# Where the four extra graph heads of a two-layer graph and product-key network stand: rounds 2, 4, 6, 8 in place of rounds 1 to 4

## The chip, the cores and the metric

The kernel runs on one core of one Trainium2 chip. The metric is the device time of one execution in microseconds, as the median of several runs; lower is better. The engines are TensorE (PE; its weight loads are shown apart as PEld), VectorE (DVE), ScalarE (ACT), GpSimd (POOL) and SyncE (SP).

## The reference

A residual stream x of 2048 rows by 128 goes through four blocks, each fed by a layer norm. The change concerns the first two alone.

```python
# 1. graph attention, 4 heads of 32, over the whole 2048 x 2048 adjacency
h = (x @ W).reshape(n, heads, head_dim)
e = src[:, :, None] + dst.T[None, :, :]
e = jnp.where(e > 0, e, ALPHA * e)
attn = softmax(where(adj > 0, e, NEG_INF));  out = layernorm(attn @ h) * gamma + beta
# 2. product keys: top 16 of 128 by top 16 of 128, then the top 16 of the 256 pairs, for each of 8 heads
k = jnp.einsum('bnhk,bnhkd->bnhd', kv_scores, keys_table[ind])
v = jnp.einsum('bnhk,bnhkd->bnhd', kv_scores, values_table[ind])
# causal attention of 8 heads of 128 over those k and v, then @ Wo
# 3. a second graph mix with one score per node; 4. a routed two-layer network of 32 experts
```

## The kernel before, in words

The 2048 rows are 16 tiles of 128. Four kinds of work belong to a tile.

**Graph heads.** Four heads a tile, numbered 4 x tile + s. A head is shown on PE (`show_head`, lines 755 and 756, eight matmuls into the PSUM tile wide), bent on ACT (line 962), reduced on DVE (`graph_logits`, line 1172), exponentiated on ACT (line 968), then transposed and multiplied on PE (`sum_head`: transposes at line 696, copies on ACT at line 910, products at line 705). After a tile's fourth head the tile is closed (`close_graph` on DVE: a compare over the next adjacency tile at line 1374, then a layer norm, a sum and a second layer norm, line 1089). `turn_xn1` on PE (line 850) turns the normed rows, and ACT copies them to xn1T.

**Picks.** For each tile four steps of key products (PE line 799) and two top-16 searches (DVE, `pick_keys`, `pick_pairs`, `pick_rows`, `pick_weights`). They need that tile's xn1T and give the row numbers idxT of its gather.

**Gathers.** POOL fetches the chosen table rows of a tile with 128 indirect DMAs (line 626). Four of them fill one slot of `ring`, a buffer of four slots. Two slots are a *pair*; a tile has 16 pairs. PE multiplies a slot by its weights (`sum_pair`, line 677) and so frees it, and only then may POOL fill the slot again. So POOL can be two pairs ahead of PE and no more.

**Attention.** Tile q attends to tiles 0 to q-1 in the steps, two of the eight heads in each (PE line 812, DVE line 1200, ACT line 1011, PE lines 696 and 705), and to itself in `own_keys`.

The order on every engine is written out by one plan, `plan_steps`, which all five engines walk in the same order. After a start that works on tiles 0 to 2, round n (n from 1 to 15) holds: the own keys of tile n-1, four steps that do the attention of tile n and the picks of tile n+1, and an end item. Its 16 pairs of gathered rows are those of tile n. Each step may also carry one graph head (`g`). Heads 12 to 63 are placed in rounds 1 to 12: four a round in the four steps, and in four rounds a fifth in a step of its own, the *extra step*, which stands ahead of the four and has no attention and no picks. `counts` says which of a step's three places takes a pair: in a round with an extra step the four steps take 2, 2, 2 and 3 pairs and the extra step 2, in a round without one they take 2, 3, 3 and 3; the own keys take 2 and the end item 3 in every round.

Where the fourth head of a tile stands in step s = 3, its closing is done inside the next round's own keys (`close=s < 3`, `left`). Where it stands in an earlier step or in the extra step, an end item without any pair follows that step at once, and the closing is done there:

```python
        g_end = g // 4 if g is not None and g % 4 == 3 else None
        if g_end is not None or k_end is not None or any(end):
            add("end", end, (1,), g=g_end if close else None, k=k_end)
```

In such an end item PE shows the next head first, which waits for line 1374 of the closing, and then waits for the last norm at `turn_xn1`:

```python
                if it["ahead"] is not None:
                    show_head(it["ahead"])
                if g is not None:
                    turn_xn1(g)
```

Of the kernel before, what the change touches and what calls it, by code (L numbers as in the profile page):

```python
# [22 lines left out]
def plan_steps(tiles):  # L23

    items, pending, count = [], [], dict(pair=0, kept=0, heads=0, met=0)

    def add(kind, fetch, turn_at, **what):  # L30
        item = dict(kind=kind, fetch=[], turn={}, kept=count["kept"], heads=count["heads"], met=count["met"], **what)
        for place, wanted in enumerate(fetch):
            if place in turn_at:
                item["turn"][place] = list(pending)
                count["kept"] += len(pending)
                pending.clear()
            item["fetch"].append(count["pair"] if wanted else None)
            if wanted:
                count["pair"] += 1
                if count["pair"] % 2 == 0:  # L40
                    pending.append(count["pair"] // 2 - 1)
        assert len(pending) <= 2
        items.append(item)

    def graph(g, fetch):
        add("graph", fetch, (1, 3), g=g)
        count["heads"] += 4
        add("end", [0, 0, 0], (1,), g=g, k=None)

    def step(fetch, g=None, k=None, q=None, s=0, end=(0, 0, 0), close=True):  # L50
        add("step", fetch, (1, 2), g=g, k=k, q=q, s=s)
        count["heads"] += g is not None
        count["met"] += 2 if q else 0
        g_end = g // 4 if g is not None and g % 4 == 3 else None
        k_end = k // 4 if k is not None and k % 4 == 3 else None
        if g_end is not None or k_end is not None or any(end):
            add("end", end, (1,), g=g_end if close else None, k=k_end)
        return None if close else g_end

    def own(d, fetch, g):  # L60
        add("own", fetch, (0, 1), d=d, g=g)

    graph(0, [0, 0, 0, 0, 0])
    for s in range(4):
        step([0, 0, 0], k=s)
    graph(1, [1, 1, 1, 1, 1])
    for s in range(4):
        left = step([1, 0, 1], g=8 + s, k=4 + s, q=0, s=s, end=[1, 1, 1] if s == 3 else (0, 0, 0), close=False)
    g = 12
    for n in range(1, tiles):  # L70
        own(n - 1, [1, 1], left)
        extra = 1 <= n <= 4
        counts = [[1, 0, 1], [1, 1, 0], [1, 1, 0], [1, 1, 1]] if extra else [[1, 0, 1], [1, 1, 1], [1, 1, 1], [1, 1, 1]]
        if extra:
            step([1, 0, 1], g=g)
            g += 1
        for s in range(4):
            k = 4 * (n + 1) + s
            left = step(counts[s], g=g if g < 4 * tiles else None, k=k if k < 4 * tiles else None, q=n, s=s,
                        end=[1, 1, 1] if s == 3 else (0, 0, 0), close=s < 3)  # L80
            g += 1
        assert count["pair"] == 16 * (n + 1)
    own(tiles - 1, [0, 0], left)
    for it, after in zip(items, items[1:]):

        it["ahead"] = after["g"] if after["kind"] == "step" and it["kind"] != "graph" else None
    items[-1]["ahead"] = None
    return items


def build_network(nc, x, adj, W, WT, a, gamma, beta, WqpkT, pkT, Wq, kv_table, Wo, Hv,
# [13 lines left out]
    SLOPE = 0.2  # L105
    CH = N // 512
    plan = plan_steps(T)

    chunks_to = [0, 0]
# [1337 lines left out]
```

## Time and profile before

| | |
|---|---|
| median of 3 runs | 3279.63 us (3275.05 to 3288.53) |
| the profiled execution | 3283.77 us, its span 3282.0 us |
| PE busy | 2180.5 us, 66% of the span |
| DVE busy | 1779.5 us, 54% |
| ACT busy | 1041.6 us, 32% |
| POOL busy | 1995.3 us, 61% |
| moved by DMA | 348.21 MB, mean 106 GB/s |

The profiled execution took 4.1 us more than the median. A share of the span is an average over the start, 15 rounds and the last two blocks, so the rows below cut the span into rounds. A round's stretch begins with the first of the 128 gathers of its tile.

### The profile page before, as it was taken

To read this page: it belongs to the slowest core of one execution; us is meant where nothing else is said; L and a number is where in the kernel's file an instruction comes from. 1 tells how busy PE (TensorE), PEld (TensorE's weight loads), DVE (VectorE), ACT (ScalarE), POOL (GpSimd) and SP (SyncE) were. 2 spreads that over 40 slices of the span, in tenths; PEclk is the share of its full clock that TensorE was granted. 3 is DMA by queue.
4 is the path that set the end of the run, shared out by engine and by line. 5 is a ranking of instruction groups with operands and counts; after the bars stand their busy time and mean duration, and the time that the engine had idled before them with its cause. 6 is when DMAs were issued, how large, how long until landed. Compare 5 with 4: busy or idle time off the path is not lost.

```text
span 3282.0 us, 42226 instructions
## 1 busy us (share of the span) xinstructions
PE 2180.5 (66%) x14008; PEld 1507.6 (46%) x14066; DVE 1779.5 (54%) x6185; ACT 1041.6 (32%) x1966; POOL 1995.3 (61%) x2078
## 2 busy tenths in 40 slices
PE   5255555656666666767676868686867676856776
PEld 4134443434344444545454645554645454534555
DVE  3737373555547565656565746565646363125444
ACT  3133232323233333333333424342423232323333
POOL 0066766676676777777777777767677777740000
PEclk8677676677778787879887978897988787977888
DMA  2033433343343434343434343434343434341110
GB/s 58 15 103 96 132 109 114 107 119 115 96 139 91 139 109 139 109 139 110 139 110 136 108 132 106 137 103 122 95 120 109 126 103 124 109 121 68 58 58 20
DMA packets 164633, 348.21 MB, mean 106 GB/s; under 512 B 38816, under 2 KB 91712, under 8 KB 160192
## 3 DMA queue, kind: packets, MB, share of 16 engines
q0 software_dynamic: 98624, 269.62, 28.6%
q1 hardware_dynamic: 65792, 75.90, 7.2%
q8 instruction: 112, 1.84, 0.2%
q14 instruction: 105, 0.86, 0.1%
HBM read 333.83 MB, written 11.53 MB: 105 GB/s over the span
## 4 chain that ended last, share of the span: by engine, by line
PE 33%; DVE 25%; POOL 18%; issue 10%; ACT 8%; DVEq 3%; DMA 2%; SPq 0%; ACTq 0%; POOLq 0%
POOL ring L626 18%; PE acc L705 11%; PE turn L696 5%; PE wide L812 4%; DVE kv L1172 3%; PE rowsum L677 2%; DMA ring<-in_kv_table,idxT 2%; ACT att_p L962 2%; ACT pt_sb L910 2%; PE wide L756 2%; DVE att_m L1200 2%; DVE pos L1243 1%; DVE sims L1235 1%; PE wide L755 1%; DVE pos L1237 1%
## 5 line engine op out<-in xcount | busy, mean ns | idle before, releaser
L626 POOL DMA_INDIRECT ring<-in_kv_table,idxT x2048 | 1984.7, 969 | 927.2 <-issue 603.1
L705 PE MATMUL acc<-kv,pt_sb 128*128 128x128 f32 x3968 | 605.5, 306 | 111.0 <-ACT pt_sb L910 110.5
L705 PEld LDWEIGHTS acc<-kv,pt_sb 128*128 128x128 f32 x3968 | 548.8, 215 | 160.1 <-ACT pt_sb L910 160.1
L677 PE MATMUL rowsum<-ring,w_block 128*32 128x256 f32 x4096 | 342.2, 441 | 358.3 <-DMA ring<-in_kv_table,idxT 353.1
L910 ACT ACTIVATE pt_sb<-turn 128x512 f32<-128x512 f32 (+2 forms) x608 | 327.6, 562 | 411.1 <-PE turn L696 410.4
L812 PE MATMUL wide<-kv,qT 128*128 128x512 f32 (+3 forms) x576 | 279.9, 623 | 129.0 <-DVE gs L1172 88.2
L677 PEld LDWEIGHTS rowsum<-ring,w_block 128*32 128x32 f32 x4096 | 104.5, 117 | 560.6 <-DMA ring<-in_kv_table,idxT 400.1
L1200 DVE TENSOR_REDUCE att_m<-wide 128x1 f32<-128x128 f32 (+14 forms) x120 | 147.0, 1225 | 205.5 <-PE wide L812 200.1
L696 PE MATMUL turn<-ident,kv 128*128 128x128 f32 x1280 | 210.1, 304 | 64.7 <-ACT kv L386 24.5
L696 PE MATMUL turn<-ident,att_p 128*128 128x128 f32 x960 | 166.6, 310 | 110.1 <-ACT kv L924 98.0
L812 PEld LDWEIGHTS wide<-kv,qT 128*128 128x128 f32 x576 | 116.2, 219 | 267.7 <-issue 267.7
L1172 DVE CUSTOM_DVE_ANT_0 kv<-wide,att_p 128x2048 f32<-128x2048 f32 x56 | 128.3, 2291 | 196.3 <-ACT att_p L962 188.0
L331 POOL DMA_DIRECT2D out<-ring x4 | 3.1, 772 | 353.0 <-DVE ring L494 353.0
L696 PEld LDWEIGHTS turn<-ident,kv 128*128 128x128 f32 x1280 | 167.6, 158 | 96.2 <-issue 64.8
L696 PEld LDWEIGHTS turn<-ident,att_p 128*128 128x128 f32 x960 | 127.9, 160 | 140.6 <-ACT kv L924 112.7
L1155 DVE TENSOR_TENSOR w_block<-wT,row_head 128x128 f32<-128x128 f32 x128 | 37.1, 291 | 268.1 <-PE rowsum L677 265.0
L917 ACT ACTIVATE sums_sb<-rowsum 128x256 f32<-128x256 f32 x128 | 48.7, 381 | 418.5 <-PE rowsum L677 418.5
L962 ACT ACTIVATE att_p<-wide,src 128x2048 f32<-128x2048 f32 x56 | 110.1, 1966 | 187.9 <-PE wide L756 187.9
L968 ACT ACTIVATE kv<-kv,gs 128x2048 f32<-128x2048 f32 x64 | 128.0, 2000 | 106.0 <-DVE gs L1175 106.0
L1020 ACT ACTIVATE top_e<-top_d 128x32 f32<-128x32 f32 x64 | 14.7, 229 | 453.3 <-DVE top_d L1245 453.3
L1011 ACT ACTIVATE att_p<-wide,att_nm 128x128 f32<-128x128 f32 (+14 forms) x120 | 133.6, 1113 | 15.1 <-DVE att_nm L1202 14.8
L756 PE MATMUL wide<-kv,sel_head 96*128 96x512 bf16 x256 | 113.2, 442 | 20.6 <-DVE kv L1374 12.3
(228 smaller groups left out, 3184.5 us busy)
## 6 DMA issues: line engine op xcount, KB each, us to landing
kv<-in_adj SPq DMA_DIRECT2D x32, 1024.0 KB, 5.0
ring<-in_kv_table,idxT POOLq DMA_INDIRECT x2048
wq_pair<-in_Wq SPq DMA_DIRECT2D x64, 128.0 KB
v_dram<-sums_sb SPq DMA_DIRECT2D x128, 64.0 KB
kv<-v_dram SPq DMA_DIRECT2D x16, 512.0 KB, 4.1
att_p<-in_Wo SPq DMA_DIRECT2D x16, 512.0 KB, 5.5
xt<-in_x SPq DMA_DIRECT2D x16, 64.0 KB
x_dram<-x SPq DMA_DIRECT2D x16, 64.0 KB, 2.0
```

Source lines behind the costliest of these rows:

```text
L626: pool.indirect_dma_start(ring[:, slot, i, :], None, kv_table, bass.IndirectOffsetOnAxis(idxT[:, r % 3, u:u + 1], 0))\
L677: mm = pe.matmul(rowsum[32 * k:32 * k + 32, 0:ROW], w_block[:, at:at + 32], ring[:, slot, k, :], start=(tk == 0), stop=(tk == 3))
L696: mm = pe.transpose(turn[q % 2][:, b * P:(b + 1) * P], probs[:, col:col + P], ident[:, :])
L705: mm = pe.matmul(dst, pt_sb[:, q % 2, b * P:(b + 1) * P], rhs(4 * q + b), start=(q + b == 0), stop=(q == len(widths) - 1 and b == widths[q ...
L756: mm = pe.matmul(wide[:, cols], sel_head[:, m % STEPS, :], dst3[:, cols], start=False, stop=True)
L812: mm = pe.matmul(wide[:, c * 512:c * 512 + w * P], qT[:, h, :], kv[:, 4 * c:4 * c + w, h * P:(h + 1) * P], start=True, stop=True)
L910: act.activation(pt_sb[:, q % 2, 0:w * P], turn[q % 2][:, 0:w * P], ACT.Copy).then_inc(copied, 1)
L962: act.activation(bent, wide[:, 0:N], ACT.Relu, bias=src4[:, m // STEPS, m % STEPS:m % STEPS + 1], scale=4.0).then_inc(gat_bent, 1)
L968: act.activation(probs, probs, ACT.Exp, bias=gs[:, s, 1:2], scale=SLOPE, accum_out=gs[:, s, 2:3]).then_inc(gat_exp, 1)
L1011: act.activation(att_p[:, 0:q * P], wide[:, 0:q * P], ACT.Exp, bias=att_nm[:, h:h + 1], accum_out=att_sum[:, h:h + 1]).then_inc(p_made, 1)
L1172: dve.tensor_tensor_reduce(probs, wide[:, 0:N], bent, 1.0, -3e38, ALU.add, ALU.max, gs[:, s, 0:1]).then_inc(dst_used, 1)
L1200: dve.reduce_max(att_m[:, h:h + 1], wide[:, 0:q * P], AX)
```

## The change

One condition of the plan is another. The extra heads stood in rounds 1 to 4; now they stand in rounds 2, 4, 6 and 8.

```diff
@@ plan_steps @@
     for n in range(1, tiles):
         own(n - 1, [1, 1], left)
-        extra = 1 <= n <= 4
+        extra = n in (2, 4, 6, 8)
         counts = [[1, 0, 1], [1, 1, 0], [1, 1, 0], [1, 1, 1]] if extra else [[1, 0, 1], [1, 1, 1], [1, 1, 1], [1, 1, 1]]
```

No instruction is added or removed: every engine has as many as before, and POOL's are in the same order. From round 9 on the plan is the one of before. What moves:

| round | heads before | closing before | heads now | closing now |
|---|---|---|---|---|
| 1 | 5 | after step 2 | 4 | none inside |
| 2 | 5 | after step 1 | 5 | after step 2 |
| 3 | 5 | after step 0 | 4 | after step 2 |
| 4 | 5 | after the extra step | 5 | after step 1 |
| 5 | 4 | none inside | 4 | after step 1 |
| 6 | 4 | none inside | 5 | after step 0 |
| 7 | 4 | none inside | 4 | after step 0 |
| 8 | 4 | none inside | 5 | after the extra step |

Before, the own keys of rounds 1 and 5 to 8 (and of 9 to 13) also close a tile; now those of rounds 1, 2 and 9 to 13 do. So four closings stood inside rounds 1 to 8 before, and seven stand there now.

PE at the start of round 1, before the change, from the last of the eight matmuls that show head 12 on: a whole step (pair, head 12, pair) comes ahead of the first step with attention.

```order
231 L756 MATMUL wide<-kv,sel_head 128x512
232 L677 MATMUL rowsum<-ring,w_block 32x256 x8
233 L686 MATMUL turn<-ident,sums_sb 128x128
234 L696 MATMUL turn<-ident,kv 128x128 x8
235 L705 MATMUL acc<-kv,pt_sb 128x128 x4
236 L696 MATMUL turn<-ident,kv 128x128 x4
237 L705 MATMUL acc<-kv,pt_sb 128x128 x4
238 L696 MATMUL turn<-ident,kv 128x128 x4
239 L705 MATMUL acc<-kv,pt_sb 128x128 x8
240 L677 MATMUL rowsum<-ring,w_block 32x256 x8
```

The same place on PE after the change:

```order
231 L756 MATMUL wide<-kv,sel_head 128x512
232 L793 MATMUL turn<-xn1T,wq_pair 128x128 x2
233 L799 MATMUL turn<-mix_keys,xn1T 128x512
234 L677 MATMUL rowsum<-ring,w_block 32x256 x8
235 L812 MATMUL wide<-kv,qT 128x128
236 L686 MATMUL turn<-ident,sums_sb 128x128
237 L696 MATMUL turn<-ident,kv 128x128 x8
238 L705 MATMUL acc<-kv,pt_sb 128x128 x4
```

The step of its own is gone from here; head 12 stands in the first step with attention, and the same rows of a fifth head now stand at the starts of rounds 6 and 8.

PE in round 7 before the change, from the end of step 0's attention to the start of step 1:

```order
1036 L696 MATMUL turn<-ident,att_p 128x128 x7
1037 L705 MATMUL acc<-kv,pt_sb 128x128 x7
1038 L755 MATMUL wide<-kv,identb 128x512
1039 L756 MATMUL wide<-kv,sel_head 128x512
1044 L755 MATMUL wide<-kv,identb 128x512
1045 L756 MATMUL wide<-kv,sel_head 128x512
1046 L793 MATMUL turn<-xn1T,wq_pair 128x128 x2
1047 L799 MATMUL turn<-mix_keys,xn1T 128x512
1048 L677 MATMUL rowsum<-ring,w_block 32x256 x8
```

The same place after the change:

```order
1021 L696 MATMUL turn<-ident,att_p 128x128 x7
1022 L705 MATMUL acc<-kv,pt_sb 128x128 x7
1023 L686 MATMUL turn<-ident,sums_sb 128x128
1024 L755 MATMUL wide<-kv,identb 128x512
1025 L756 MATMUL wide<-kv,sel_head 128x512
1030 L755 MATMUL wide<-kv,identb 128x512
1031 L756 MATMUL wide<-kv,sel_head 128x512
1032 L850 MATMUL turn<-ident,xn_tmp 128x128
1033 L793 MATMUL turn<-xn1T,wq_pair 128x128 x2
1034 L799 MATMUL turn<-mix_keys,xn1T 128x512
1035 L677 MATMUL rowsum<-ring,w_block 32x256 x8
```

The turn of the closing (line 850) stands between the shown head and the products that begin step 1, ahead of that step's first pair.

## Rows read from the trace of the kernel before

**Rows 1.** The page: its costliest group: busy us, mean ns, then idle.

```profile
L626 POOL DMA_INDIRECT ring<-in_kv_table,idxT x2048 | 1984.7, 969 | 927.2 <-issue 603.1
```

**Rows 2.** Busy time by round, 1 to 8; columns as in the first row.

```profile
core 0: us, PE busy (x) PEld busy (x) DVE busy (x) ACT busy (x) POOL busy (x), PEclk, DMA share, GB/s
357.50:539.00 181.50, 106.53 (x671) 69.44 (x676) 101.13 (x391) 52.55 (x111) 122.82 (x128) 0.72 0.41 119
539.00:719.30 180.30, 113.27 (x694) 74.88 (x699) 96.62 (x363) 54.16 (x111) 123.36 (x128) 0.71 0.39 113
719.30:900.70 181.40, 114.84 (x718) 76.32 (x723) 97.82 (x363) 56.12 (x111) 124.51 (x128) 0.74 0.39 112
900.70:1078.50 177.80, 111.94 (x742) 75.35 (x747) 99.17 (x363) 57.26 (x111) 124.43 (x128) 0.80 0.39 114
1078.50:1243.20 164.70, 108.12 (x727) 74.94 (x731) 96.93 (x358) 53.07 (x112) 125.65 (x129) 0.80 0.42 124
1243.20:1406.70 163.50, 111.04 (x751) 75.87 (x755) 98.20 (x358) 54.70 (x112) 124.53 (x128) 0.80 0.43 124
1406.70:1569.70 163.00, 112.46 (x775) 76.41 (x779) 99.17 (x358) 56.75 (x112) 123.99 (x128) 0.85 0.43 125
1569.70:1733.30 163.60, 117.04 (x799) 80.95 (x803) 100.26 (x358) 58.38 (x112) 124.62 (x129) 0.85 0.43 124
```

**Rows 3.** POOL before its gathers (line 626), round 1: idle us, times.

```profile
  issue: 38.1, 125
  PE rowsum L677: 20.6, 3
```

**Rows 4.** The same of round 7.

```profile
  PE rowsum L677: 1.2, 4
```

**Rows 5.** Timeline of POOL: late gathers, rounds 1 to 4, idle in brackets.

```profile
498.99 0.94 POOL L626 DMA_INDIRECT ring<-in_kv_table,idxT  x1 [16.35 <-PE rowsum L677]
...
678.74 0.94 POOL L626 DMA_INDIRECT ring<-in_kv_table,idxT  x1 [2.92 <-PE rowsum L677]
...
860.32 0.94 POOL L626 DMA_INDIRECT ring<-in_kv_table,idxT  x1 [7.23 <-PE rowsum L677]
...
1037.71 0.94 POOL L626 DMA_INDIRECT ring<-in_kv_table,idxT  x1 [7.99 <-PE rowsum L677]
```

**Rows 6.** Timeline of PE, round 1: first pairs of extra step and step 0.

```profile
386.50 0.64 PE L677 MATMUL rowsum<-ring,w_block 128*32 128x256 f32 x8
...
406.43 0.64 PE L677 MATMUL rowsum<-ring,w_block 128*32 128x256 f32 x8
```

**Rows 7.** Timeline of PE, round 4: pairs 8 and 10 (steps 2 and 3).

```profile
1008.25 0.85 PE L677 MATMUL rowsum<-ring,w_block 128*32 128x256 f32 x12
...
1036.76 0.85 PE L677 MATMUL rowsum<-ring,w_block 128*32 128x256 f32 x12
```

**Rows 8.** Timeline of PE: round 5 pairs 7 and 10, round 7 pair 4.

```profile
1165.24 0.64 PE L677 MATMUL rowsum<-ring,w_block 128*32 128x256 f32 x8
...
1193.47 0.64 PE L677 MATMUL rowsum<-ring,w_block 128*32 128x256 f32 x8
...
1467.26 1.07 PE L677 MATMUL rowsum<-ring,w_block 128*32 128x256 f32 x16
```

**Rows 9.** Timeline of PE, round 8: pairs 7 and 10 (steps 2 and 3).

```profile
1659.36 0.64 PE L677 MATMUL rowsum<-ring,w_block 128*32 128x256 f32 x8
...
1689.81 0.85 PE L677 MATMUL rowsum<-ring,w_block 128*32 128x256 f32 x12
```

**Rows 10.** Who waited for a closing (line 1374), rounds 1 to 4: us, times.

```profile
  PE wide L756: 10.7, 3
```

**Rows 11.** Who waited for the closing norm (line 1089), rounds 1 to 4.

```profile
  PEld turn L850: 26.0, 4
```

**Rows 12.** PE before the pairs (line 677), waiting for rows: rounds 4, 8.

```profile
  DMA ring<-in_kv_table,idxT: 23.1, 7
...
  DMA ring<-in_kv_table,idxT: 20.5, 6
```

## The prediction, made before the changed kernel ran

> **What bounds the kernel now.** I read the page first. POOL's gathers are its largest group: 1984.7 us busy in 2048 instructions and 927.2 us idle before them, of which 603.1 us stand as issue [rows 1]. Busy plus issue is 1.26 us a gather, so 128 gathers cannot take less than some 162 us, whatever the other engines do.
>
> Then I cut the span into rounds [rows 2]. The reader is to see two kinds. Rounds 5 to 8, with four heads, take 164.7, 163.5, 163.0 and 163.6 us, though PE's busy time grows from 108 to 117 us in them: something else sets their length. Rounds 1 to 4, with five heads and less attention, take 181.5, 180.3, 181.4 and 177.8 us. Next I asked what POOL waited for. In round 7 it is 1.2 us for PE [rows 4]; the rest of its 39.0 us of idle time (163.0 less 123.99 busy) is the issue of its own gathers. In round 1 it is 38.1 us of issue, the same, and 20.6 us in three places for PE to free a slot [rows 3]. So a round costs POOL's floor, which I take as 163.3 us (10.2 us a pair), plus what PE's lateness adds to it.
>
> The lateness has a place. POOL may issue pair m+2 only once PE has started pair m. Undisturbed it issues pair m+2 at (m+2) x 10.2 us after the round's first gather, and a released gather starts 1.0 us after PE's start on the pair (1036.76 to 1037.71 us) [rows 5, 7]. PE's deadline for pair m is therefore (m+2) x 10.2 - 1.0. In all four rounds of five heads the gather that tells is the first of pair 12, released by pair 10 of step 3. It should go out 122.4 us into the round and goes out after 141.5, 139.7, 141.0 and 137.0 us [rows 2, 5]: 19.1, 17.3, 18.6 and 14.6 us late, which are the lengths of these rounds over 163.3 (18.2, 17.0, 18.1, 14.5). What PE does before pair 10 counts; what it does after, POOL's six remaining pairs cover.
>
> **Two things make PE late.** The extra step: 19.9 us from its first pair to the next step's [rows 6], in which POOL fills two pairs, 20.4 us. By itself it keeps pace, but it takes a pair from each of steps 1 and 2, which then bring two pairs (20.4 us) in 28.5 us [rows 7]. The closing inside a round: PE waits 10.7 us in three cases for the compare and 26.0 us in four for the last norm [rows 10, 11], 9.2 us a closing. It costs least after the extra step, which has neither picks nor attention. In rounds 5 to 8 I take 8 us, since attention keeps PE busy longer ahead of it. Bounds: 6.5 us, if only the wait for the norm is left (26.0 over four), and 10.1, if both stand in full (10.7 over three more).
>
> **Growth with the round.** From the second of these steps to the third it is 28.5 us with four blocks of attention (1008.25 to 1036.76) and 30.4 us with eight (1659.36 to 1689.81) [rows 7, 9]: 0.5 us a step and block. Three steps end before pair 10, so a late round grows by 1.4 us a block. Bounds: 0, as between rounds 1 and 3, where the closing also moved, and 2.0, if the extra step or the own keys grow like a fourth.
>
> **The change, round by round,** each against its length before.
>
> Round 1 gets four heads and no closing inside: the form of round 7, 163.3 us. -18.2.
>
> Round 2 gets the form of round 1 (five heads, closing after step 2) with one block more: 181.5 + 1.4 = 182.9. +2.6.
>
> Round 3 gets four heads and a closing after step 2, ahead of pair 10. In round 5 PE starts pair 10 after 115.0 us (1193.47 - 1078.50) [rows 8] against a deadline of 121.4. Of 9.2 us of closing 6.4 us are covered; 2.8 are left: 166.1. -15.3.
>
> Round 4 gets the form of round 2 with two blocks more: 180.3 + 2.8 = 183.1. +5.3.
>
> Round 5 gets a closing after step 1, ahead of pair 7. PE starts pair 7 after 86.7 us (1165.24 - 1078.50) [rows 8], deadline 90.8: 4.1 covered of 8, 3.9 left: 167.2. +2.5.
>
> Round 6 gets the form of round 3 with three blocks more: 181.4 + 4.2 = 185.6. +22.1.
>
> Round 7 gets a closing after step 0, ahead of pair 4. PE starts pair 4 after 60.6 us (1467.26 - 1406.70) [rows 8], deadline 60.2: nothing is covered, 8 us: 171.0. +8.0.
>
> Round 8 gets the form of round 4 with four blocks more: 177.8 + 5.6 = 183.4. +19.8.
>
> The sum is +26.8 us. Rounds 9 to 15 and the tail are the same program, and since each round begins in step with POOL I give them nothing. SyncE's loads and stores move with the closings; they wait on the same events as before, and no row shows PE waiting for them there. I give them nothing, at most 1 us a closing. The profiled execution's 3283.8 becomes 3310.6; it lies 4.1 us over the median, so the median becomes 3279.6 + 26.8 = 3306.
>
> **A rule of the clock.** The granted clock is 0.72, 0.71 and 0.74 in rounds 1 to 3 and 0.80 to 0.85 in rounds 4 to 8 [rows 2], a mix of stretches at 1.2 and 2.4 GHz. The Trainium skill (TensorE: Matmul & The Clock Gate, Part 1) says that PE's full clock is given by activity and taken away by idleness. By that rule the moved heads run faster in the busier rounds 6 and 8. The extra step's 19.9 us is the most that a head's PE work can be; the ratio of 0.72 to 0.85 would take at most 3.0 us from each of two, and the sum would be +20.8. I keep +26.8, as the waits between engines in that step don't follow PE's clock.
>
> **The rivals.** (a) *No change.* Heads cost a late round what they cost an early one, and a closing in a round of four heads is covered by PE's waits for rows. Then round 1 gives 18.2, round 3 18.1, round 2 takes 1.2, round 4 2.5, rounds 5 and 7 nothing, round 6 takes 17.9 and round 8 14.2: -0.5 us, 3279. For it: rounds 1 to 3 did not grow with their blocks. Against it: pair 4 of round 7 has no cover, and steps do grow. Chance 0.17.
>
> (b) *Faster.* The extra step fits into PE's waiting. PE waits 20.5 us for rows in round 8 [rows 12], and the step is 19.9 us long. If that time could be moved ahead of pair 10, rounds 6 and 8 would stay at the floor, and the sum is 26.8 - 22.1 - 19.8 = -15.1, 3264 us. It decides where the gather of pair 12 in round 8 is less than 4 us late. Against it: round 4 waits 23.1 us [rows 12] and is late all the same, since PE waits in the end item and the own keys, behind the late place. Chance 0.06.
>
> (c) *The dearer price.* Closings at 10.1 us and growth of 2.0 us a block, the covers as above. Round by round: -18.2, +3.2, -14.4, +6.5, +4.6, +23.9, +10.4, +22.2, or +38.2 us, 3318. For it: DVE, which does the closings and the picks, is as busy in rounds 5 to 8 as in rounds 2 to 4 (97 to 100 us) [rows 2], so nothing makes a closing cheaper there for sure. Chance 0.15.
>
> **How the numbers follow.** My forecast has 0.62. Its own range is 3290 to 3318: the lower end has growth 0 and closings at 6.5 us in rounds 5 and 7 (-18.2, +1.2, -15.3, +2.5, +1.0, +17.9, +6.8, +14.2, or +10.1 us), the upper one is (c). With 0.23 in (a) and (b) the whole range has to reach into (a): 3281 to 3322, where the last 4 us are for the stores and loads. Half a per cent, 16.4 us, is what a measurement of this kernel can tell from no change, so slower begins at 3296: 0.62 + 0.15, less a little for the low end of the forecast, is 0.74. Within it: 0.19. Faster: 0.07.
>
> **What would show it.** Round 1 in the new profile at 163 to 164 us with the wait of its gathers for PE near 1 us. Round 6 at 183 to 188 us and round 8 at 180 to 187, each with a gather late by 6 us or more in front of pairs 8 to 12. Round 7 at 167 to 173 us with one late gather, that of pair 6, behind the closing. Round 3 at 164 to 169. Rounds 9 to 15 as before within 1 us each. The prediction is wrong if rounds 6 and 8 stay under 170, if rounds 5 and 7 stay at the floor, or if a round past 8 moves.

## The result, and the profile after

The changed kernel takes 3310.3 us in the median of 5 runs (3306.67 to 3315.28), the kernel before 3279.63 us in runs beside it (3271.68 to 3288.53). The ratio is 1.0095, with a 95% interval from 1.0072 to 1.0118: 31 us, or 0.95%, slower. Measured once more later, the same two kernels gave 1.0086 (1.0071 to 1.0101). The profiled execution took 3310.30 us, its span 3308.6 us. The forecast was 3306 us, slower, in a range from 3281 to 3322.

Busy time by round after the change, rounds 1 to 8, with the columns of [rows 2]:

```profile
360.20:523.20 163.00, 96.70 (x615) 62.42 (x619) 90.90 (x352) 46.00 (x103) 124.01 (x129) 0.73 0.43 125
523.20:706.90 183.70, 112.45 (x695) 73.47 (x700) 103.94 (x397) 54.58 (x112) 125.13 (x128) 0.72 0.40 117
706.90:874.90 168.00, 107.41 (x663) 69.49 (x667) 94.78 (x358) 49.17 (x104) 123.72 (x129) 0.71 0.42 121
874.90:1056.70 181.80, 117.48 (x742) 78.38 (x747) 98.66 (x363) 57.33 (x111) 123.71 (x128) 0.77 0.39 112
1056.70:1224.40 167.70, 109.14 (x727) 72.39 (x731) 96.93 (x358) 53.32 (x112) 124.70 (x129) 0.80 0.42 121
1224.40:1408.60 184.20, 121.36 (x806) 84.63 (x811) 100.97 (x363) 61.60 (x119) 124.06 (x128) 0.82 0.38 111
1408.60:1578.70 170.10, 115.00 (x775) 76.51 (x779) 98.93 (x358) 56.87 (x112) 123.54 (x128) 0.82 0.41 120
1578.70:1765.20 186.50, 130.40 (x854) 90.52 (x859) 103.01 (x363) 65.25 (x119) 124.27 (x128) 0.82 0.38 109
```

The reader is to see the pattern of the plan: 163.0 us in round 1 with four heads, 183.7, 181.8, 184.2 and 186.5 us in the rounds with five, and 168.0, 167.7 and 170.1 us in rounds 3, 5 and 7, which have four heads and a closing inside. POOL's busy time is 123.5 to 125.1 us in all eight, much as before (122.8 to 125.7). Side by side with the lengths of [rows 2] and the forecast:

| round | before | forecast | after | moved |
|---|---|---|---|---|
| 1 | 181.5 | 163.3 | 163.0 | -18.5 |
| 2 | 180.3 | 182.9 | 183.7 | +3.4 |
| 3 | 181.4 | 166.1 | 168.0 | -13.4 |
| 4 | 177.8 | 183.1 | 181.8 | +4.0 |
| 5 | 164.7 | 167.2 | 167.7 | +3.0 |
| 6 | 163.5 | 185.6 | 184.2 | +20.7 |
| 7 | 163.0 | 171.0 | 170.1 | +7.1 |
| 8 | 163.6 | 183.4 | 186.5 | +22.9 |
| sum | 1375.8 | 1402.6 | 1405.0 | +29.2 |

The experiments hold a second profile of the changed kernel. In it the eight rounds take 163.2, 184.7, 168.2, 183.8, 167.7, 184.3, 170.5 and 186.1 us, together 1408.5. Six agree with the table within 0.4 us, rounds 2 and 4 are 1.0 and 2.0 us longer. So the sum is +29 us by one profile and +33 by the other, and a difference of 2 us in one round is not safe from a single profile.

The gathers of POOL that waited longest for PE after the change, one for each of rounds 2 to 8:

```profile
666.45 0.94 POOL L626 DMA_INDIRECT ring<-in_kv_table,idxT  x1 [15.98 <-PE rowsum L677]
...
834.82 0.94 POOL L626 DMA_INDIRECT ring<-in_kv_table,idxT  x1 [5.56 <-PE rowsum L677]
...
991.26 0.94 POOL L626 DMA_INDIRECT ring<-in_kv_table,idxT  x1 [15.44 <-PE rowsum L677]
...
1152.76 0.94 POOL L626 DMA_INDIRECT ring<-in_kv_table,idxT  x1 [4.28 <-PE rowsum L677]
...
1313.76 0.94 POOL L626 DMA_INDIRECT ring<-in_kv_table,idxT  x1 [8.40 <-PE rowsum L677]
...
1477.86 0.94 POOL L626 DMA_INDIRECT ring<-in_kv_table,idxT  x1 [7.85 <-PE rowsum L677]
...
1724.25 0.94 POOL L626 DMA_INDIRECT ring<-in_kv_table,idxT  x1 [10.36 <-PE rowsum L677]
```

Rounds 3, 5 and 7 each have one such gather, of 5.56, 4.28 and 7.85 us: those of pairs 12, 9 and 6, each the second pair behind the one that PE takes after the closing. That is their excess over the floor of 163.3 us within 1.1 us. Round 1 has none over 0.31 us, where the row at 498.99 us stood before [rows 5].

Rounds 9 to 15 before and after, in one stretch each (the first row is of before, the second of after):

```profile
1733.30:2918.20 1184.90, 870.46 (x5753) 601.33 (x5769) 624.37 (x2119) 393.01 (x768) 865.66 (x897) 0.85 0.40 116
```

```profile
1765.20:2945.10 1179.90, 862.89 (x5753) 593.67 (x5769) 623.77 (x2119) 393.31 (x768) 865.95 (x897) 0.86 0.40 117
```

They are 5.0 us shorter after, though their program is the same. Single rounds moved by up to 2.3 us either way: round 9 is 2.0 us longer, rounds 10 and 12 are some 2.3 us shorter. The prediction had said within 1 us each, and had named a round past 8 that moves as a sign of being wrong; this sign went against it. Whether the change moved them is open. For it: the second profile of the changed kernel takes 1180.2 us there, and each of its rounds is within 0.4 us of the first profile's. Against it: among the nine profiles with four slots and these same rounds (two of the changed kernel, one of the kernel before, six of other kernels below) the value is 1179.2 to 1184.9 us and doesn't follow the placement. The placement of before has 1179.2 with the lighter closing and 1184.4 with the spread pairs. The kernel before has but one profile.

The start up to round 1, also the same program, took 357.5 us before and 360.2 after, 359.5 in the second profile, and 355.8 to 360.5 us in the other kernels with four slots. The 2.7 us lie within this spread and aren't put down to the change.

### The profile page after: what moved, and what is told of

It reads as the page before. It is cut to its first block, busy times and chain, and to the rows that moved or that the text cites. A ratio compares the mean times of both kernels' runs of the same rounds, so it can differ in the third digit from the quotient of the medians.

```text
span 3308.6 us, 42229 instructions
## 1 busy us (share of the span) xinstructions
PE 2190.4 (66%) x14008; PEld 1504.6 (45%) x14066; DVE 1777.8 (54%) x6185; ACT 1043.2 (32%) x1966; POOL 1995.1 (60%) x2078
## 3 DMA queue, kind: packets, MB, share of 16 engines
q0 software_dynamic: 98624, 269.62, 28.5%
## 4 chain that ended last, share of the span: by engine, by line
PE 30%; POOL 23%; DVE 23%; issue 11%; ACT 8%; DVEq 3%; DMA 2%; SPq 0%; ACTq 0%; POOLq 0%
POOL ring L626 23%; PE acc L705 9%; PE turn L696 4%; PE wide L812 4%; DVE kv L1172 2%; PE rowsum L677 2%; DMA ring<-in_kv_table,idxT 2%; ACT pt_sb L910 2%; DVE att_m L1200 2%; ACT att_p L962 2%; PE wide L756 2%; DVE pos L1243 1%; DVE sims L1235 1%; DVE scratch L1212 1%; DVE pos L1237 1%
## 5 line engine op out<-in xcount | busy, mean ns | idle before, releaser
L910 ACT ACTIVATE pt_sb<-turn 128x512 f32<-128x512 f32 (+3 forms) x608 | 327.5, 562 | 413.5 <-PE turn L696 412.9
L1172 DVE CUSTOM_DVE_ANT_0 kv<-wide,att_p 128x2048 f32<-128x2048 f32 x56 | 128.3, 2291 | 185.6 <-ACT att_p L962 178.3
L1020 ACT ACTIVATE top_e<-top_d 128x32 f32<-128x32 f32 x64 | 14.7, 229 | 455.0 <-DVE top_d L1245 455.0
```

The source lines that it names most:

```text
L910: act.activation(pt_sb[:, q % 2, 0:w * P], turn[q % 2][:, 0:w * P], ACT.Copy).then_inc(copied, 1)
L1172: dve.tensor_tensor_reduce(probs, wide[:, 0:N], bent, 1.0, -3e38, ALU.add, ALU.max, gs[:, s, 0:1]).then_inc(dst_used, 1)
```

## The experiments

Ratios are to the kernel before, run beside each kernel, with a 95% interval. Lengths of rounds are of the profiled execution.

### The extra steps in rounds 5 to 8

```diff
-        extra = n in (2, 4, 6, 8)
+        extra = n in (5, 6, 7, 8)
```

> The extra steps stand in rounds 5 to 8; the four closings inside a round are those of before (after step 2, 1, 0 and after the extra step), moved four rounds on. My theory (a fifth head costs a round what makes PE late at pair 10, and that grows by 1.4 us for each block of attention): rounds 1 to 4 at 163.3 us, rounds 5 to 8 at 187, 186, 187 and 186.5 us, in all 24 us over before, about 3303 us. Rival A (all of the change's loss is the three added closings, and a fifth head costs the same in any round): as before, 3280 us. Rival B (the loss is that heads in late rounds are dear, and closings cost nothing): the four heads are moved further than in the change (by 16 rounds together, not by 10), so the loss is 1.6 times the change's 31 us, about 3329 us.

Measured: 3304.91 us, ratio 1.0056 (1.0035 to 1.0077). That is some 18 us more, where 24 were expected (1.007, inside the interval). Both rivals' ratios, 1.000 and 1.015, lie outside. Rounds 5 to 8:

```profile
1017.60:1203.40 185.80, 119.43 (x783) 83.20 (x788) 107.36 (x397) 60.08 (x120) 126.50 (x129) 0.79 0.39 116
1203.40:1386.60 183.20, 122.31 (x806) 85.07 (x811) 100.93 (x363) 61.54 (x119) 125.24 (x128) 0.81 0.38 111
1386.60:1573.20 186.60, 123.54 (x830) 84.76 (x835) 102.05 (x363) 63.56 (x119) 124.94 (x128) 0.84 0.37 109
1573.20:1758.40 185.20, 129.00 (x854) 89.26 (x859) 102.91 (x363) 65.31 (x119) 123.85 (x128) 0.83 0.37 110
```

The same forms took 181.5, 180.3, 181.4 and 177.8 us in rounds 1 to 4 [rows 2], so four blocks more cost 4.3, 2.9, 5.2 and 7.4 us, 1.2 us a block. The four closings inside are the same four, so these 19.8 us are what the later place costs. Rounds 1 to 4 take 162.5 to 166.1 us, 3.1 us more together than rounds 5 to 8 did before. In all, rounds 1 to 8 take 22.8 us more (1398.6 us), with no closing added. So dearer late rounds make one part of the change's loss. That closings inside more rounds make the other part, the next pair of kernels has to show.

### A lighter closing, in both placements

```diff
-                norm(ln_tmp[:, :], g_out[:, :])
+                if light:
+                    dve.tensor_copy(ln_tmp[:, :], g_out[:, :])
+                else:
+                    norm(ln_tmp[:, :], g_out[:, :])
...
                 if g is not None:
-                    close_graph(g)
+                    close_graph(g, light=g > 1)
```

> The kernel before, but the closings that stand in an end item inside a round leave out their first layer norm and copy the rows instead (so that norm is missing from four tiles' results). The norm and its drains take about 3.6 us on DVE, the copy 0.3. My theory (PE waits for the closing before the pair that POOL waits for): 3.3 us less in each of rounds 1 to 4, 13 us in all, about 3266 us. Rival (closings are covered, the fifth head alone is the cost): no change, 3280 us.

> The changed kernel with the same lighter closing, in its seven end items inside a round (the first norm is missing from seven tiles' results). My theory: 3.3 us less in each of rounds 2 to 8, 23 us in all, about 3287 us, and the distance to the lighter kernel before falls from 31 to 21 us. Rival (closings in rounds of four heads are covered): only rounds 2, 4, 6 and 8 gain, 13 us, about 3297 us. Rival (closings cost nothing anywhere): 3310 us.

Measured: the kernel before with it 3269.54 us, ratio 0.9957 (0.9942 to 0.9971), 14 us less. The changed kernel with it 3282.12 us, ratio 0.9990 (0.9978 to 1.0003). The distance between the placements falls from 0.95% to 0.33%, or 11 us (5 to 17 by the two intervals) where 21 were expected. In rounds 1 to 8 of the profiles it falls from 29.2 to 15.9 us: the kernel before gives back 10.7 us there, the changed one 24.0, where 13 and 23 were expected. By the ratios the changed kernel gives back more, 1.05% or 34 us. The changed kernel itself was not run beside this one, so the size rests on the profiles. Rounds 3, 5 and 7 of the changed kernel with it:

```profile
703.70:868.40 164.70, 107.60 (x663) 69.60 (x667) 92.56 (x344) 49.19 (x104) 123.97 (x129) 0.72 0.42 123
...
1047.30:1211.40 164.10, 105.31 (x727) 70.78 (x731) 94.67 (x344) 53.25 (x112) 124.89 (x128) 0.82 0.41 124
...
1391.90:1558.00 166.10, 114.27 (x775) 77.75 (x779) 96.75 (x344) 57.08 (x112) 124.73 (x128) 0.84 0.41 122
```

They fall by 3.3, 3.6 and 4.0 us, as rounds 2, 4, 6 and 8 do by 3.5, 2.9, 3.7 and 3.1 us. So closings are paid for in rounds of four heads too, and the rival by which those are covered falls.

### Fewer pairs at the end of a round with an extra step

```diff
-        counts = [[1, 0, 1], [1, 1, 0], [1, 1, 0], [1, 1, 1]] if extra else [[1, 0, 1], [1, 1, 1], [1, 1, 1], [1, 1, 1]]
+        counts = [[1, 0, 1], [1, 1, 1], [1, 1, 1], [1, 1, 1]]
+        last = [1, 0, 0] if extra else [1, 1, 1]
...
-                        end=[1, 1, 1] if s == 3 else (0, 0, 0), close=s < 3)
+                        end=last if s == 3 else (0, 0, 0), close=s < 3)
```

> The kernel before, but in rounds with an extra step the four steps take 2, 3, 3 and 3 pairs as in the other rounds, and the end item takes 1 pair in place of 3. Same work, same heads, same closings. My theory (what costs is that pair 10 comes late in the order, not that the engines have too much to do): rounds 1 to 4 fall from 181.5, 180.3, 181.4 and 177.8 us to 165, 167, 169 and 165, about 55 us less, 3225 us. Rival (a round of five heads is as long as its chain on PE, DVE and ACT, however the pairs are spread): rounds 1 to 4 as before, 3280 us.

> The changed kernel with the pairs of its rounds 2, 4, 6 and 8 spread as 2, 3, 3, 3 in the steps and 1 in the end item. My theory: these rounds fall from 183.7, 181.8, 184.2 and 186.5 us to 166, 170, 172 and 170, some 58 us less, about 3252 us. Rival (the chain of the engines sets these rounds): no change, 3310 us.

Measured: with the placement of before 3242.29 us, ratio 0.9873 (0.9854 to 0.9893), 42 us less where 55 were expected; with that of the change 3260.23 us, ratio 0.9924 (0.9907 to 0.9941), 56 us below the change by the two ratios, where 58 were expected. The profiles give less: 48 us in rounds 1 to 8, since rounds 2, 4, 6 and 8 fall by 51 us and rounds 3, 5 and 7 grow by 4. No engine's work changed. Rounds 1 to 4 of the first kernel stood 68 us over the floor together and lose 39 of them, so the rival (the chain of the engines sets these rounds) falls for these 39 and is not refuted for the other 28. Rounds 1 to 4 of the first:

```profile
355.80:524.60 168.80, 102.83 (x671) 67.72 (x676) 101.26 (x391) 52.47 (x111) 125.42 (x129) 0.75 0.42 127
524.60:697.40 172.80, 112.51 (x700) 76.03 (x704) 96.86 (x364) 54.16 (x111) 124.37 (x129) 0.72 0.40 118
697.40:868.80 171.40, 114.77 (x722) 76.18 (x723) 97.78 (x364) 56.09 (x111) 124.69 (x128) 0.76 0.40 119
868.80:1037.40 168.60, 115.15 (x747) 78.73 (x747) 99.32 (x364) 57.34 (x111) 124.19 (x129) 0.79 0.41 121
```

For these 165, 167, 169 and 165 us were expected. What POOL waited for in round 2, with idle us and times, says what is left:

```profile
  issue: 38.1, 125
  PE rowsum L678: 6.9, 2
  ACT idxT L1045: 4.1, 2
```

POOL's wait for PE has gone from 18.9 us in the kernel before to 6.9 us, and a new wait of 4.1 us stands beside it, for the row numbers of the next tile (idxT), which the picks give at the end of the round. With only one pair left in the end item POOL runs up to that point. In the changed placement with this spread, rounds 3, 5 and 7 take 168.4, 169.4 and 171.8 us, 0.4 to 1.7 us more than without it.

### Five slots in the ring, in both placements

```diff
-    SLOTS = 4
+    SLOTS = 5
...
-        wT = sb("wT", [P, 3, P])
-        idxT = sb("idxT", [P, 3, P], U32)
+        wT = sb("wT", [P, 2, P])
+        idxT = sb("idxT", [P, 2, P], U32)
...
-        beta_b = sb("beta_b", [P, P])
-        hv_b = sb("hv_b", [P, P])
+        beta_b = gamma_b
+        hv_b = gamma_b
```

> The kernel before with five slots in the ring in place of four, so that POOL may be two and a half pairs ahead. To make room, wT and idxT have two buffers in place of three, beta and Hv stand in gamma's tile and are not loaded (the results are not the reference's), and some small tiles share their place. The order of the work is the same. My theory (the cost is POOL waiting for a slot): each late place is 5 us less late, so rounds 1 to 4 lose 5 us each, the start and rounds 9 to 15, which are late too, some 30 us together, about 3230 us. Rival (the rounds are as long as the chain on PE, DVE and ACT): 3280 us.

> The changed kernel with the same five slots. My theory: rounds 2, 4, 6 and 8 lose 5 us each, rounds 3, 5 and 7, which are 5, 4 and 7 us over the floor, lose that or 5 us, and the late rounds as much as in the other kernel: about 3247 us, so that the distance between the two placements falls from 31 to about 17 us. Rival (work is dearer where it now stands, by the clock or by what runs beside it, whatever POOL may fill): the distance stays at 31 us.

The edit also takes one of three buffers from wT and idxT, puts some tiles in one place and leaves out two loads, the same in both placements. Measured: before with five slots 3240.80 us, ratio 0.9874 (0.9858 to 0.9889); the change with five slots 3252.81 us, ratio 0.9915 (0.9903 to 0.9928). The distance falls from 0.95% to 0.41%, or 13.5 us (7 to 20 by the two intervals), near the 17 expected and far from the rival's 31. Rounds 3, 5, 7 and 8 of the changed placement with five slots:

```profile
699.60:863.10 163.50, 105.87 (x663) 69.00 (x667) 94.85 (x358) 49.13 (x104) 124.28 (x128) 0.73 0.42 124
...
1041.40:1204.70 163.30, 102.04 (x727) 68.79 (x731) 97.06 (x358) 52.97 (x112) 124.30 (x129) 0.84 0.42 125
...
1386.20:1551.50 165.30, 110.73 (x775) 75.63 (x779) 98.95 (x358) 56.62 (x112) 124.70 (x129) 0.85 0.42 123
1551.50:1733.00 181.50, 130.12 (x854) 90.67 (x859) 103.08 (x363) 65.28 (x119) 124.53 (x129) 0.83 0.39 112
```

Rounds 3, 5 and 7 are at or near the floor: a closing's lateness of 4 to 8 us is covered up to the 5 us that one slot adds. Round 8 falls from 186.5 to 181.5. Rounds 1 to 4 of the placement of before with five slots:

```profile
354.90:532.50 177.60, 103.74 (x671) 67.76 (x676) 100.88 (x391) 52.69 (x111) 125.95 (x128) 0.73 0.41 121
532.50:709.60 177.10, 112.17 (x694) 73.35 (x699) 96.57 (x363) 54.13 (x111) 124.50 (x128) 0.71 0.39 115
709.60:887.90 178.30, 116.53 (x718) 78.24 (x723) 97.73 (x363) 56.11 (x111) 124.63 (x129) 0.72 0.39 114
887.90:1064.70 176.80, 116.67 (x742) 79.26 (x747) 98.78 (x363) 57.37 (x111) 124.22 (x129) 0.78 0.39 115
```

They lose 3.9, 3.2, 3.1 and 1.0 us, where I had expected 5 each. The traces say why less: PE itself reaches pair 10 later in these rounds, by 0.7, 1.9, 1.8 and 4.2 us. In round 4 it starts it 140.2 us into the round, where it was 136.1 [rows 7]:

```profile
1028.07 1.07 PE L675 MATMUL rowsum<-ring,w_block 128*32 128x256 f32 x16
```

One slot more is worth half a pair, 5.1 us; less these delays that is 4.4, 3.2, 3.3 and 0.9 us, what was measured within 0.5 us. Which part of the edit delays PE wasn't tried. In rounds 2, 4, 6 and 8 of the changed placement PE is later by 0.5, 1.4, 2.2 and 0 us, 4.1 us together against 8.6. So the delays themselves bring the placements nearer: rounds 1 to 8 differ by 14.7 us here, and by an estimate from these starts would differ by some 19 without them.

### The extra steps in rounds 1, 3, 5 and 7

```diff
-        extra = n in (2, 4, 6, 8)
+        extra = n in (1, 3, 5, 7)
```

> The extra steps stand in rounds 1, 3, 5 and 7, each one round earlier than in the change. Six closings stand inside rounds 1 to 8 (after step 2 in 1 and 2, step 1 in 3 and 4, step 0 in 5 and 6, the extra step in 7). My theory, put together from rounds of the same form measured so far: 181.5, 167, 181.5, 166.5, 184, 169.5, 184.5 and 163.6 us, in all 22 us over before, about 0.3% below the change in the same call. Rival (the loss comes from heads and closings taking turns with rounds without them): as the change, 31 us over before.

> The changed kernel itself, on the same chip as the others of this call, as the measure for them: 0.95% over before. Rival: some of the 0.95% was the chip of that day, and it is under 0.7% or over 1.2% here.

Measured: 3312.30 us, ratio 1.0088 (1.0074 to 1.0102), and the changed kernel beside it 3309.59 us, ratio 1.0086 (1.0071 to 1.0101), so its loss repeats. I had expected the odd placement 9 us under the change, and it isn't: this run went the rival's way. Rounds 2, 4 and 6, the ones with four heads and a closing inside:

```profile
539.40:706.60 167.20, 98.68 (x639) 62.03 (x643) 93.60 (x358) 47.82 (x104) 124.18 (x129) 0.73 0.42 122
...
889.90:1058.30 168.40, 110.62 (x687) 70.71 (x691) 95.80 (x358) 51.01 (x104) 124.30 (x129) 0.74 0.42 121
...
1241.70:1413.50 171.80, 114.05 (x751) 78.80 (x755) 98.10 (x358) 54.97 (x112) 124.72 (x129) 0.81 0.41 118
```

They are 167.2, 168.4 and 171.8 us against 167, 166.5 and 169.5 that I had taken; round 3 has 183.3 against 181.5. Each round is within 2.3 us of its form measured elsewhere. But five are longer and two a little shorter, and rounds 3, 4, 6 and 8, each 1.1 to 2.3 us over, make the 7 us by which the sum is over. Two placements that differ by one round and one closing can't be told apart by this sum, and it doesn't rule out that taking turns has a small cost of its own.

### Rounds 9 to 15 as well, and a pair in the closing

```diff
+        if n >= 9:
+            counts[0], last = [1, 1, 1], [1, 0, 1]
```

> The kernel before with the spread of pairs of the experiment above in rounds 1 to 4, and besides in rounds 9 to 15 a pair more in step 0 (3 in place of 2) and one less in the end item. These rounds are late at pair 6 by 1.8, 5.6, 4.0, 8.3, 1.3, 4.3 and 2.9 us before. My theory: 55 us less in rounds 1 to 4 and some 20 us less in rounds 9 to 15, about 3205 us. Rival (the late rounds are as long as PE's chain): 3225 us, as with rounds 1 to 4 alone.

Measured: 3208.35 us, ratio 0.9767 (0.9753 to 0.9782), 76 us less where 75 were expected. The parts were not as expected: rounds 9 to 15 take 1145.9 us together, 39 us less than before and not 20, while rounds 1 to 4 give 40 us and not 55, so the agreement of the sum is in part luck. Rounds 9 to 15 stood 42 us over seven floors of 163.3 us before. For the 20 us I had counted only the wait at pair 6 of each round, 28 us in all; the gathers of pairs 9, 12 and 15 waited another 23 us for PE.

The next kernel adds a pair to the end item of a closing inside and takes it from the step behind (after the extra step in the same way, with `counts[0]`):

```diff
+            if s < 3 and g < 4 * tiles and g % 4 == 3:
+                counts[s + 1], inside = [0, 1, 1], [1, 0, 0]
...
-                        end=last if s == 3 else (0, 0, 0), close=s < 3)
+                        end=last if s == 3 else inside, close=s < 3)
```

> The kernel of the last experiment (the placement of before, pairs spread in rounds 1 to 4 and 9 to 15), and besides each end item that does a closing inside a round takes a pair, the first of the step behind it, so that PE frees the slot before it waits for the closing. My theory: rounds 1 to 4, at 168.2, 170.6, 173.9 and 168.7 us, lose the 3 to 5 us that the closing still makes them late, some 14 us together, 0.4% below the kernel without this. Rival (these rounds are now as long as the chain on PE, DVE and ACT): no change against it.

> The kernel with pairs spread in rounds 1 to 4 and 9 to 15 again, on the same chip as the kernel with a pair in the closing, as the measure for it: 2.3% under before.

Measured: 3193.67 us, ratio 0.9733 (0.9715 to 0.9751), beside 3209.11 us and 0.9774 (0.9759 to 0.9789) for the kernel without it: 0.42% less, as expected. Rounds 1 to 4 without it:

```profile
358.30:526.50 168.20, 106.72 (x671) 70.42 (x676) 101.00 (x391) 52.71 (x111) 124.85 (x128) 0.72 0.44 128
526.50:696.90 170.40, 110.28 (x699) 73.50 (x704) 97.18 (x364) 54.26 (x111) 125.31 (x129) 0.75 0.41 120
696.90:870.90 174.00, 117.02 (x722) 77.86 (x723) 98.05 (x364) 56.02 (x111) 125.23 (x128) 0.74 0.41 117
870.90:1039.60 168.70, 113.36 (x746) 76.36 (x747) 99.33 (x364) 57.22 (x111) 123.95 (x128) 0.80 0.42 121
```

And with it:

```profile
359.60:527.60 168.00, 103.91 (x671) 68.88 (x680) 101.20 (x391) 52.60 (x111) 124.40 (x128) 0.76 0.44 129
527.60:690.50 162.90, 109.03 (x698) 71.67 (x695) 96.87 (x364) 54.27 (x111) 123.24 (x128) 0.75 0.43 124
690.50:856.30 165.80, 112.46 (x722) 75.09 (x727) 97.77 (x364) 55.86 (x111) 124.62 (x128) 0.78 0.42 123
856.30:1029.30 173.00, 118.01 (x748) 79.96 (x752) 99.80 (x364) 57.23 (x111) 124.70 (x129) 0.80 0.41 118
```

The sum of the four falls by 11.6 us, but not as I had thought: rounds 2 and 3 lose 7.5 and 8.2 us and reach the floor or nearly, round 1 stays, and round 4, whose closing stands after the extra step, becomes 4.3 us longer. Step 0 has one pair of three places there; whether that is what costs it wasn't tried. This kernel does all the work of the one before, is 2.7% faster than it, and 3.5% faster than the change.

## Why the prediction was right

**What bounds the kernel.** POOL's floor and PE's lateness at a deadline gave the lengths; the kernels with spread pairs added the wait for idxT. The cleanest test is the spread of pairs, which took 42 us out without touching any engine's work. The other is the fifth slot, which lets POOL run further ahead and took the distance between the placements from 31 to 13.5 us; its edit also delays PE, so by the estimate above some 5 us of this fall aren't the slot's.

**The forms.** The forecast of a round from a round of the same form, or of four heads and a closing, was right within 1.4 us in rounds 1, 2, 4, 5, 6 and 7 (2.0 by the second profile). The sum was 2.4 us under the 29.2 us measured, or 5.9 under the second profile's. From span to span the profiles are 26.6 us apart, almost the forecast's 26.8. That is luck: the start's 2.7 us more and the 5.0 us less of rounds 9 to 15, which I gave nothing, work against each other and against the 2.4. The medians are 30.7 us apart, since the profiled execution before lay 4.1 us over its median and the one after on it.

**The closing in a round of four heads** came out right in rounds 5 and 7 by two errors against each other, which is luck too. PE's starts on pairs 2 and 4 of round 7 after the change:

```profile
1438.21 0.64 PE L677 MATMUL rowsum<-ring,w_block 128*32 128x256 f32 x8
...
1476.47 1.45 PE L677 MATMUL rowsum<-ring,w_block 128*32 128x256 f32 x12
```

And on pair 2 of round 7 before, with pair 4 in [rows 8]:

```profile
1440.32 1.05 PE L677 MATMUL rowsum<-ring,w_block 128*32 128x256 f32 x13
```

From pair 2 to pair 4 it is 38.3 us now and was 26.9: the closing costs PE 11.3 us, not 8. The waits named at it,

```profile
  PE wide L756: 1.2, 1
```

```profile
  PEld turn L850: 7.7, 1
```

for the compare and for the last norm, are 8.9 us, near my 8; the other 2.4 us are not in these waits, and I took them for nothing; where they arise I have not shown. But pair 2 starts 29.6 us into the round and not 33.6. The own keys no longer close a tile; that this gives the 4.0 us is my reading and wasn't tried. I gave that relief nothing either. In rounds 5 and 7 the two cancel. In round 3 they don't. PE's starts on its pairs 7 and 10:

```profile
792.65 0.85 PE L677 MATMUL rowsum<-ring,w_block 128*32 128x256 f32 x12
...
833.43 1.08 PE L677 MATMUL rowsum<-ring,w_block 128*32 128x256 f32 x8
```

Pair 7 starts 85.8 us into the round, as in round 5 before (86.7), since PE has waited for rows in between and lost the relief; from there to pair 10 it is 40.8 us, against 28.2 before [rows 8]. So pair 10 comes 126.5 us into the round, 5.1 us after its deadline where I had 2.8, and the gather of pair 12 waits 5.56 us. That term was short by 2 us: round 3 has 168.0 for 166.1.

**Growth with the round** was 1.4 us a block in the forecast (a block is the attention of one more tile). By the four forms it was 2.2, 0.8, 0.9 and 2.2 us a block (rounds 2, 4, 6 and 8 against their models; round 4 gives 1.8 by the second profile), and 1.2 in the mean of the experiment with rounds 5 to 8. The size for round 8, the form whose closing stands after the extra step, was off: 8.7 us for 5.6, and 7.4 us in the experiment. It misses by 3.1 us, the largest miss of a term. The traces say where: against round 4 before, PE in round 8 after takes 3.6 us more from pair 4 to pair 6, 2.3 from pair 6 to 8 and 2.1 from pair 8 to 10. I had read the growth off the last of these three steps and taken 0.5 us a block for each; the step right behind the closing grows by 0.9. Why it does is open.

**The clock rule.** The granted clock in round 1 is 0.73 with four heads and was 0.72 with five; in rounds 5 to 8 it is 0.80 to 0.82. These are means of whole rounds. The extra step's own stretch, from its first pair to the next step's, is another matter. In rounds 6 and 8 after the change:

```profile
1252.60:1271.10 18.50, 13.23 (x96) 9.17 (x96) 3.16 (x6) 8.46 (x10) 13.93 (x16) 0.82 0.40 113
1607.10:1636.00 28.90, 15.38 (x97) 10.16 (x97) 13.10 (x43) 10.12 (x13) 21.89 (x24) 0.74 0.50 151
```

Before, these stretches had 0.74, 0.74, 0.82 and 0.74 in rounds 1 to 4. So an extra step had 0.82 in the busier round 6, as the Trainium skill (TensorE: Matmul & The Clock Gate, Part 1) would have it, but 0.74 in round 8, whose mean is 0.82 as well. The length hardly follows the clock: without a closing it is 19.9 and 19.6 us at 0.74, and 19.4, 19.1, 19.9 and 18.5 at 0.82 or 0.83; with the closing it is 28.5 us in round 4 before and 28.9 in round 8 after, both at 0.74. The 3.0 us that I had allowed each of the two by this rule aren't there, and its sum, +20.8 us, is further from the 29.2 measured than the one without it. No run changes the clock by itself.

**The rivals.** (a), no change, falls with rounds 5 and 7, which have 3.0 and 7.1 us more, and with the growth of rounds 6 and 8. (b), faster, would have needed the gather of pair 12 in round 8 less than 4 us late; it was 10.36 us late, behind two others. (c) had the closing nearer to its true price on PE (10.1 us for 11.3) but no relief in the own keys beside it, and too much growth in rounds 4 and 6; its sum was 9 us too high. What (b) pointed at was real, though: the idle time of PE at the end of a round can be used, but by moving pairs away from it, not by moving heads.

## What to carry to other kernels

Where one engine fills a short ring (a buffer of few slots, used in turn) for another, write down each consumer's deadline along the order of work. A round's length is then the floor plus the worst lateness, and one can say from the old profile what a moved piece will cost in its new place. The order of the consumer's takes is then worth more than the place of the extra work: spreading 16 takes evenly over the same work gave 42 us, and with the late rounds and the closings 2.7%, where the placement of the extra heads moved 0.9%. Look then for the next wait in line, here the row numbers that a round's end gives to the next gather.

## What the runs showed of the hardware

The issue of indirect gathers is steady: the median gather keeps POOL busy for 0.95 us and the next starts 0.30 us after its end, in rounds at the floor and late ones, with four slots or five. Of the 2048 gathers 113 to 144 took longer than 1.05 us, up to 2.0. The start of one and the same program took 359.5 and 360.2 us up to round 1 in the two profiles of the changed kernel, with a first stretch of 128 gathers of 181.6 and 184.5 us. The other kernels with four slots show the same two values for this stretch, within 0.2 us, though their program up to there is the same. What sets the one or the other, the runs don't show.
